# Layer norm of six of eight batches of x made on ScalarE in three passes, in a fused cross-attention and feed-forward kernel

## What is computed

```python
def _layernorm(x, axis=-1, eps=1e-05):
    m = jnp.mean(x, axis=axis, keepdims=True)
    v = jnp.var(x, axis=axis, keepdims=True)
    return (x - m) / jnp.sqrt(v + eps)
...
    x = x + xattn(_layernorm(x), ctx, Wq, bq, Wk, bk)   # Q = text Wq^T + bq, K = ctx Wk^T + bk,
                                                        # softmax(Q K^T / 32) ctx
    x = x + ffn(_layernorm(x), qweight, qzeros, scales, bias, g_idx)   # x W + bias, W unpacked from 4 bits
```

## Time and profile before

| | |
|---|---|
| median of 3 runs | 554.11 us (554.05 to 554.15) |
| the profiled execution, its own time | 553.43 us |
| its span in the profile | 551.6 us |
| TensorE busy | 542.7 us, 98% |
| VectorE busy | 385.6 us, 70% |
| ScalarE busy | 239.1 us, 43% |
| GpSimd busy | 184.5 us, 33% |

### The profile page before, as it was taken

The page is one execution under the profiler, slowest core; times in us unless marked ns, Lnnn a source line. Parts: engine busy times, 40 slices in busy tenths (PEclk is TensorE's granted clock), DMA queues, the critical chain, the costliest instruction groups (busy, mean ns, idle before and its releaser), DMA issues.

```text
span 551.6 us, 7449 instructions
## 1 busy us (share of the span) xinstructions
PE 542.7 (98%) x2702; PEld 454.9 (82%) x2702; DVE 385.6 (70%) x644; ACT 239.1 (43%) x426; POOL 184.5 (33%) x139
## 2 busy tenths in 40 slices
PE   8999999999999999999999999999999999999997
PEld 7888888887777767778889999998788888888886
DVE  4987776689889997894213555574777789778742
ACT  6964344411431341342427666676463253334210
POOL 1071000010000000000225977777667545743630
PEclk9999999999999999999999999999999999999999
DMA  8852100349677845744344799998427776774311
GB/s 291 289 167 64 38 1 0 116 159 315 213 204 260 227 191 177 224 165 158 116 159 185 259 358 351 318 402 328 198 81 241 214 230 228 229 228 126 106 76 76
DMA packets 47411, 107.08 MB, mean 194 GB/s; under 512 B 3632, under 2 KB 24184, under 8 KB 45200
## 3 DMA queue, kind: packets, MB, share of 16 engines
q1 hardware_dynamic: 40848, 100.33, 51.9%
q10 hardware_dynamic: 6528, 6.29, 5.4%
HBM read 66.70 MB, written 39.85 MB: 193 GB/s over the span
## 4 chain that ended last, share of the span: by engine, by line
PE 69%; DVE 15%; DMA 7%; ACT 5%; issue 3%; POOL 1%; ACTq 0%; SPq 0%; DVEq 0%; POOLq 0%
PE bank L1242 16%; PE bank L1244 16%; PE bank L1243 16%; PE bank L1286 5%; PE bank L1292 5%; PE bank L1289 5%; DMA xq<-xn_scratch 3%; PE bank L1346 2%; DVE xq L953 2%; DVE junk L1008 2%; DVE stats L918 2%; DMA right_scratch<-part_hi 2%; DVE xT_lo L859 2%; DVE part_t L1047 1%; DMA xn_scratch<-xin 1%
## 5 line engine op out<-in xcount | busy, mean ns | idle before, releaser
L1242 PE MATMUL bank<-xT_hi,m_hi 128*128 128x512 f32 x256 | 101.3, 396 | 1.6 <-DVE xT_lo L859 1.6
L1244 PE MATMUL bank<-xT_hi,m_lo 128*128 128x512 f32 x256 | 99.7, 390 | 0.0
L1243 PE MATMUL bank<-xT_lo,m_hi 128*128 128x512 f32 x256 | 99.7, 389 | 0.0
L751 ACT ACTIVATE t_pair<-bank,ucol 128x512 f32<-128x512 f32 x32 | 22.0, 686 | 100.4 <-PE bank L1244 100.4
L1194 DVE TENSOR_TENSOR xres<-xres,bank 128x512 f32<-128x512 f32 x56 | 38.2, 682 | 36.2 <-PE bank L1244 36.0
L550 POOL TENSOR_TENSOR tT_lo<-t_pair,tT_hi 128x1024 fp32r<-128x1024 f32 x16 | 38.1, 2399 | 73.7 <-ACT tT_hi L592 73.7
L1242 PEld LDWEIGHTS bank<-xT_hi,m_hi 128*128 128x128 f32 x256 | 48.0, 188 | 14.1 <-issue 2.5
L529 POOL TENSOR_TENSOR pairs<-mv,pairs 128x2 f32<-128x2 f32 x8 | 5.6, 695 | 161.0 <-DVE mv L927 161.0
L564 POOL TENSOR_TENSOR l_lo_s<-l_sum_s,l_hi_s 128x512 fp32r<-128x512 f32 x32 | 40.5, 1298 | 56.0 <-DVE l_sum_s L1135 56.0
L1244 PEld LDWEIGHTS bank<-xT_hi,m_lo 128*128 128x128 f32 x256 | 48.0, 188 | 10.2
L1243 PEld LDWEIGHTS bank<-xT_lo,m_hi 128*128 128x128 f32 x256 | 48.1, 188 | 9.9 <-issue 0.2
(11 more groups left out here) (145 smaller groups left out, 1244.0 us busy)
## 6 DMA issues: line engine op xcount, KB each, us to landing
cin<-in_ctx SPq DMA_DIRECT2D x8, 1024.0 KB, 5.7
xres<-in_x SPq DMA_DIRECT2D x8, 1024.0 KB, 11.5
out<-xres SPq DMA_DIRECT2D x15, 512.0 KB, 5.9
right_scratch<-part_hi SPq DMA_DIRECT2D x28, 256.0 KB, 2.2
xn_scratch<-xin SPq DMA_DIRECT2D x6, 1024.0 KB, 5.0
xq<-xn_scratch ACTq DMA_DIRECT2D x24, 256.0 KB, 5.7
r_tile<-right_scratch SPq DMA_DIRECT2D x6, 1024.0 KB, 12.0
yn_scratch<-yin SPq DMA_DIRECT2D x6, 1024.0 KB, 4.0
```

The lines of the kernel that those rows point to most:

```text
L1242: pe.matmul(out_, a_hi, b_hi, start=start, stop=False, skip_group_check=True)
L1243: pe.matmul(out_, a_hi, b_lo, start=False, stop=False, skip_group_check=True)
L1244: return pe.matmul(out_, a_lo, b_hi, start=False, stop=stop, skip_group_check=True)
```

## The change

Batches 2 to 7 of x are normalised on ScalarE, with another arithmetic. A pass with Copy sums each row (`accum_out`), a tiny instruction makes the negative mean, a pass with Square and that mean as its bias sums the squared differences, and a third pass multiplies by rstd and adds shift = -mean * rstd. GpSimd makes three small instructions for a batch (scale and eps, power, shift) where it made one. The results of the first two passes that nobody reads go to two tiles, xjunk, laid over s3 and zz. So the first pass waits until the eight DMAs that read s3 and zz have landed (`s_placed`). The third pass waits for row sums explicitly (`s_dot`), since they are now on another engine. The places n in the tables stay as they are, but they now count in ScalarE's loop, ahead of the rounding and of the eviction of the same n.

```diff
+        xjunk = [at(f"xjunk{t}", 188.25 + 2 * t, [P, D], BF16) for t in range(QT)]
...
             def rsqrt(n):
-                pool.wait_ge(s_stat, n + 1)
-                if n < B:
+                if n < 2:
+                    pool.wait_ge(s_stat, n + 1)
+                elif n < B:
+                    pool.wait_ge(s_xsq, QT * (n - 1))
+                    pool.tensor_scalar(mv[:, :, 1], xsquares, 1.0 / D, EPS, ALU.mult, ALU.add).then_inc(s_xvar, 1)
+                    pool.wait_ge(s_xvar, n - 1)
+                else:
+                    pool.wait_ge(s_stat, n - B + 3)
+                if n < 2:
                     pool.tensor_tensor(rstd, mv[:, :, 1], power, ALU.pow).then_inc(s_rstd, 1)
                 else:
                     pool.tensor_tensor(rstd, mv[:, :, 1], power, ALU.pow).then_inc(s_rpow, 1)
-                    pool.wait_ge(s_rpow, n - B + 1)
+                    pool.wait_ge(s_rpow, n - 1)
                     pool.tensor_tensor(shift, nmean, rstd, ALU.mult).then_inc(s_rstd, 1)
...
+            def x_stats(b):
+                act.wait_ge(s_xraw[b % 2], 16 * (b // 2))
+                if b == 2:
+                    act.wait_ge(s_placed, 16 * 8)
+                    act.wait_ge(s_rstd, 2)
+                for t in range(QT):
+                    act.activation(xjunk[t], raw_rows(b)[:, t, :], ACT.Copy, accum_out=xsum[:, t:t + 1]).then_inc(s_xsum, 1)
+                act.wait_ge(s_xsum, QT * (b - 1))
+                act.activation(nmean, xsum, ACT.Copy, scale=-1.0 / D).then_inc(s_xmean, 1)
+                act.wait_ge(s_xmean, b - 1)
+                for t in range(QT):
+                    act.activation(xjunk[t], raw_rows(b)[:, t, :], ACT.Square, bias=nmean[:, t:t + 1],
+                                   accum_out=xsquares[:, t:t + 1]).then_inc(s_xsq, 1)
+
+            def x_apply(b):
+                act.wait_ge(s_rstd, b + 1)
+                if b == 2:
+                    act.wait_ge(s_xtr, NB)
+                else:
+                    act.wait_ge(s_xst, 16 * (b - 2))
+                act.wait_ge(s_dot, b)
+                for t in range(QT):
+                    act.activation(by_quadrant(xin[:, 1, t, :]), raw_rows(b)[:, t, :].rearrange("q (k a i) -> q k a i", k=NB, a=4),
+                                   ACT.Identity, bias=shift[:, t:t + 1], scale=rstd[:, t:t + 1]).then_inc(s_xn, 1)
+
             act.wait_ge(s_cons, 2)
+            x_stats(2)
             for p in range(PAIRS):
                 for j in range(NB):
                     n = NB * p + j
+                    if n in X_STATS:
+                        x_stats(X_STATS[n])
+                    if n in X_APPLY:
+                        x_apply(X_APPLY[n])
...
             row_terms(0)
             row_terms(1)
-            x_stats(2)
             for p in range(PAIRS):
...
-                    if n in X_STATS:
-                        x_stats(X_STATS[n])
-                    if n in X_APPLY:
-                        x_apply(X_APPLY[n])
```

More of the change, by code:

```diff
@@ L97, in xattn_ffn_kernel @@
         shift = at("shift", 1.15625, [P, QT], F32)
+        xsum = at("xsum", 1.1875, [P, QT], F32)
+        xsquares = at("xsquares", 1.21875, [P, QT], F32)
         m_hi = at("m_hi", 1.75, [P, NB, D], F32R)
@@ L215, in xattn_ffn_kernel @@
         s_xl = [sem(f"x_loaded{i}") for i in range(2)]
+        s_xsum, s_xmean, s_xsq, s_xvar = sem("x_summed"), sem("x_mean"), sem("x_squares_summed"), sem("x_variance")
         s_stat, s_rstd, s_xn, s_dot = sem("ln_stats"), sem("ln_rstd"), sem("xn_done"), sem("row_terms")
@@ L929, in x_stats @@
             def x_stats(b):
[L930 to L935, removed]
+                dve.wait_ge(s_xl[b], 16)
+                ln_stats(xin[:, b, :, :])
             def x_apply(b):
                 dve.wait_ge(s_rstd, b + 1)
[L939 to L942, removed]
                 for t in range(QT):
[L944 to L948, removed]
+                    rows = xin[:, b, t, :]
+                    dve.tensor_scalar(rows, rows, mv[:, t, 0:1], rstd[:, t:t + 1], ALU.subtract, ALU.mult).then_inc(s_xn, 1)
             def x_blocks(b):
```

## The result

The changed kernel takes 560.74 us (median of 5 runs, 560.29 to 562.72), the kernel before 554.11 us (median of 5 runs now). It is 6.6 us slower. The ratio of the mean times is 1.0127, 95% interval 1.0113 to 1.0142. The profiled execution has a span of 558.9 us against 551.6.

A forecast was written before the change was run, and what follows sets the result against it. TensorE, busy 542.7 us of a 551.6 us span, was taken as the bound. The second pair 9.2 us late less 2.4 us of waits won gave +6.8 us, on the median 560.9 us; range 557.0 to 566.0.

The forecast's parts named there:

- The start: ScalarE's first pass over batch 2 waits for the eight placing DMAs and starts at 114.4 us; bounds 113.9 and 115.5.
- One batch on ScalarE and GpSimd: From first pass to normalised batch 8.65 us: statistics 4.95, GpSimd 1.3, third pass 2.4; VectorE and GpSimd took 5.3.
- The first gather: TensorE, ready to gather at 129.64, waits 6.5 us for the one-hot matrix, ready at 136.2 behind batch 3's row sums.
- The reading back: Moves of normalised batches 2 and 3 start together after 132.35; batch 3 is back at 152.0, between 149.1 and 153.0.
- The second pair: TensorE starts it at 156.2 us and not 147.0, 9.2 us late; bounds 6.5 to 10.5.
- the DMA chain: Batch 3 normalised, stored, read back, block-transposed, then first xT_lo done: second pair at 156.2 us.
- half speed: If a 6.5 us wait slows TensorE's clock, it loses 3.0 us, reaches the second pair at 156.5; time 561.2 us.
- the wait of 1 to 4 us: Sign expected in TensorE's timeline at the second pair's first matmul, put down to xT_lo.
- What was won: TensorE's four second-stage waits for VectorE go, 2.4 us; bounds 1.9 to 2.4, the last 0.30 us least sure.
- Later batches at nothing: In the second and third pair ScalarE's passes fit its gaps and cost nothing; up to 2 us if cover failed.
- The rival "faster": The placing DMAs don't bind; first pass by 107.9, neither chain late, 2.4 us won, 551.7 us; chance 0.07.
- "nearly" saturated: VectorE in the second stage is nearly saturated and ScalarE is not, so moving work may pay; prize 2.4 us.

The follow-up runs named there:

- the one with the load put back: Against the changed kernel, VectorE got back as much work as it lost for batches 4 to 7, on an unread tile: 563.3 us, kernel before 553.04.
- the first pass at 107.48: Against the changed kernel, SyncE issued the eight placing DMAs ahead of the load of batch 3: 552.23 us, kernel before 553.04.

## Why the prediction was right

It said 560.9 us for a median of 554.11 before, and the measured median is 560.74. Step by step, with the 0.75 us of the later start of the stage taken off:

- **The start.** Forecast 114.4, measured 115.24, that is 114.5. The last placing DMA decides it.
- **One batch on ScalarE and GpSimd.** Forecast 8.65 us, measured 115.24 to 123.81, 8.57. The statistics were put at 4.95, though the terms named there add up to 5.03 (4.54 + 0.2 + 0.29), and took 4.84; the Copy passes are 1.04 to 1.06 us, a little less than the row with a per-partition factor; GpSimd's three instructions and their handing over took 1.36 us (forecast 1.3), and the scaling cost 0.2 us like the shift.
- **The first gather.** Forecast 6.5 us of wait, measured 6.39.
- **The reading back.** Forecast batch 3 back at 152.0, measured 152.65, that is 151.9. The bounds were 149.1 and 153.0, and the choice of 152.0 between them was a judgement; that it hit to 0.1 us is in part luck, for its story was not quite right. The reads of batch 2 were to start behind the third pass of batch 3 and an eviction. ScalarE's queue issued three of the four at 130.47, as that pass began, and the last at 131.85, though both passes and the eviction stand ahead of them in the queue; the rows stand below this list. The four were back at 138.16, and the store of batch 3 took 7.4 us (132.87 to 140.3) where it had taken 5.5.
- **The second pair.** Forecast 9.2 us late by the DMA chain or 9.5 by TensorE itself if it ran at half speed. Measured 10.0, that is 9.25. Half speed came, and the two chains ended together, within 0.2 us. So the wait of 1 to 4 us that was to show at the second pair did not show, which was one of the prediction's own signs: half speed, which was given no chance of its own, took up the time. The forecast stood because the two sums, with half speed and without, had come out 0.3 us apart.
- **What was won.** Forecast 2.4, measured 2.27; 0.17 us of the last wait stayed, the one that was called least sure. The sum closes: 6.4 of wait, 2.6 of half speed and the 0.2 at the pair, less 2.3, are 6.9 us, and the medians differ by 6.6.
- **Later batches at nothing.** Right: no eviction and no rounding made TensorE wait, and the kernel with batches 4 to 7 alone shows it without the loss.

The timeline of ScalarE in the changed kernel at the reading back of batch 2 (the issues are ACTq). The ACTIVATEs ran in the order of the queue, but the first DMA issues ran ahead of the second pass, and all four ahead of the eviction, though both stand before them in the queue:

```profile
130.47 1.35 ACTq L740 DMA_DIRECT2D xq<-xn_scratch  x3
131.61 1.22 ACT L765 ACTIVATE xin<-xin,shift,pairs 128x1024 f32<-128x1024 f32 x1
131.85 0.47 ACTq L740 DMA_DIRECT2D xq<-xn_scratch  x1
132.74 1.82 ACT L792 ACTIVATE t_pair<-bank,ucol 128x512 f32<-128x512 f32 x3
```

The rule of the Trainium skill ("TensorE: Matmul & The Clock Gate", section "Why this matters for your kernels"), that a long idle gap puts the array back to 1.2 GHz, held in this trace (0.50 granted from 135.8 on). By the rows it hardly changed the time: VectorE's first xT_lo instruction ran from 156.18 to 156.9, so the DMA chain would have held TensorE for as long. That is argued from these rows; no kernel took the half speed away alone. The rival "faster" was right in its mechanism: with the first pass at 107.48, ahead of the 107.9 from which it was said to decide, the first gather is on time. It was wrong that neither chain would be late then, since the reading back had lost its lead. The advice of the Trainium skill ("Perfetto Trace Analysis", section "Optimizing Scalar/DVE Operations"), that work may go from a saturated VectorE to ScalarE, agrees with the kernel that moves batches 4 to 7 alone: VectorE was busy 46.8 of the 50 us from 150 to 200 in the kernel before, and that move won 2.7 us. Over the whole stage VectorE was busy 76%, which is less than the "nearly" saturated of the prediction.

## What to carry to other kernels

Before work moves to an idle engine, look at what it must wait for there that it didn't wait for before; here a scratch tile, laid over a source that eight late DMAs still read, cost some 9 us (6.6 lost and 2.3 not won), where all there was to win was 2.4. Look also for what stands in the old engine's queue behind the moved result: VectorE was idle and the pick was ready to go, but in order. And where two chains come out level, an edit that frees one of them shows little; find the start they share, or move only the part that has slack (batches 4 to 7 here).

## What the runs showed of the hardware

A long wait of TensorE cost more than its length here. In six kernels, after waits of 3.3 to 6.4 us, the granted clock fell to 0.50 between 2.2 and 5.3 us after TensorE's last matmul, still within the wait, and each of these stretches at 0.50 lasted 6.8 us: 135.8 to 142.6 in the changed kernel, 134.9 to 141.7 in the one with the load put back, 132.6 to 139.4 and 133.2 to 140.0 in the two with a wait added, 143.5 to 150.4 with the first pick earlier, 151.3 to 158.1 with the block transpose later as well. What was left of the stretch when TensorE went back to work cost it a little under half of that: 1.4 us after a wait of 6.3, 2.7 us after one of 3.3. The waits of 1.37 us and less left the clock at 1.00.

The reading of ScalarE's accumulator (0.19 us) starts 0.97 us into a pass of 1.06, and the next pass starts 0.09 later, so summing passes over 1024 columns follow each other every 1.06 us (115.24 and 116.30 in the changed kernel). No run has the same pass without the sum. On GpSimd the power of 128x2 elements takes 0.69 us, a multiply or a scaling of the same 0.20.
